# Row scatters without their pacing waits, and expert biases loaded as rows and turned on TensorE, in an attention and mixture-of-experts layer

## What is computed

```python
x = layernorm(x + attention(x))          # 8 heads of 64, causal, gated per head
x = layernorm(x + ffn(x))
# ffn: 16 experts with hidden width 256, two chosen for each token, and a shared network of width 512
logits = x @ Wg;  gates = softmax over the two largest logits
y = sum over chosen e: gates[e] * ((silu(x @ W1[e] + b1[e]) * (x @ W11[e] + b11[e])) @ W2[e] + b2[e])
z = silu(x @ Ws1 + bs1) * (x @ Ws11 + bs11) @ Ws2 + bs2
ffn = y + z
```

## Time and profile before

| | |
|---|---|
| time, median of 3 runs | 671.99 us (671.56 to 672.36) |
| time of the profiled execution | 674.43 us |
| its span, first to last instruction | 672.7 us |
| PE busy | 626.1 us (93%) |
| DVE, ACT, POOL busy | 456.1, 387.4, 176.8 us |
| shared network, first product to last | about 491 to 559 us of the span |
| experts | about 559 to 645 us |

### The profile page before, as it was taken

One profiled execution on the slowest core, in us unless ns is written; L12 is line 12 of the kernel. 1 busy time (PEld: TensorE's weight loads), 2 busy tenths in 40 slices (PEclk: granted clock), 3 DMA queues, 4 the chain that ended last, 5 costly groups with the idle time before them and its releaser, 6 DMA issues.

```text
span 672.7 us, 14853 instructions
## 1 busy us (share of the span) xinstructions
PE 626.1 (93%) x5286; PEld 506.0 (75%) x5286; DVE 456.1 (68%) x1493; ACT 387.4 (58%) x821; POOL 176.8 (26%) x302
## 2 busy tenths in 40 slices
PE   7899999999999999999999999999996979888865
PEld 5688888778888877888887788888754548778752
DVE  5977767677776767777676787767684355556524
ACT  6766556676655667665566766556551114656643
POOL 5211101231110122111012211101336633666640
PEclk9999999999999999999999999999997979999997
DMA  7499961179970119993011200000293112222224
GB/s 156 109 168 158 167 96 33 34 145 167 174 116 2 32 33 66 4 5 2 1 34 32 64 1 2 2 1 1 75 313 49 43 33 71 72 71 73 63 66 153
DMA packets 112920, 48.55 MB, mean 72 GB/s; under 512 B 53712, under 2 KB 106192, under 8 KB 112848
## 3 DMA queue, kind: packets, MB, share of 16 engines
q1 hardware_dynamic: 109456, 42.20, 43.0%
q0 software_dynamic: 2560, 5.28, 2.3%
q10 hardware_dynamic: 832, 0.14, 0.1%
HBM read 14.78 MB, written 24.43 MB: 58 GB/s over the span
## 4 chain that ended last, share of the span: by engine, by line
PE 81%; DVE 8%; ACT 4%; issue 2%; another core or an unknown queue 2%; DMA 1%; DVEq 0%; ACTq 0%; POOLq 0%; POOL 0%; SPq 0%
PE ps_o L1304 19%; PE ps_t L1166 18%; PE ps_s L1270 10%; PE ps_s L1272 9%; PE ps_s L1438 6%; PE ps_o L1426 3%; PE ps_s L1348 2%; PE ps_o L1166 2%; PE ps_o L1316 2%; PE ps_s L1177 2%; PE ps_s L1174 2%; PE ps_t L1362 2%; DVE q_hl L821 1%; PE ps_s L1456 1%
## 5 line engine op out<-in xcount | busy, mean ns | idle before, releaser
L1166 PE MATMUL ps_t<-ident,probs 128*128 128x128 f32 x1104 | 172.8, 273 | 4.8 <-ACT probsT L690 2.0
L1166 PEld LDWEIGHTS ps_t<-ident,probs 128*128 128x128 f32 x1104 | 135.8, 140 | 43.8 <-issue 8.3
L679 ACT ACTIVATE probs<-probs,nmax 128x128 f32<-128x128 f32 (+15 forms) x128 | 153.4, 1199 | 22.9 <-DVE nmax L977 15.9
L986 DVE COPY probsT<-ps_t 128x512 f32<-128x512 f32 (+3 forms) x160 | 91.2, 570 | 100.5 <-PE ps_t L1166 99.2
L690 ACT ACTIVATE probsT<-ps_t 128x512 f32<-128x512 f32 (+3 forms) x160 | 89.3, 558 | 95.3 <-PE ps_t L1166 94.1
L1270 PE MATMUL ps_s<-k_h,q_hl 128*128 128x512 f32 (+3 forms) x320 | 141.0, 444 | 0.4 <-DVE q_hl L821 0.4
L1304 PE MATMUL ps_o<-probsT,v_sb 128*64 128x128 f32 x2176 | 140.0, 277 | 0.1
L549 POOL TENSOR_TENSOR rden<-rsum,minus_one 128x2 f32<-128x2 f32 x64 | 44.3, 693 | 348.8 <-ACT probs L679 337.6
L972 DVE TENSOR_SCALAR_CACHE_REDUCE probs<-ps_s 128x512 f32<-128x512 f32 x192 | 127.7, 686 | 0.3 <-issue 0.3
L1304 PEld LDWEIGHTS ps_o<-probsT,v_sb 128*64 128x64 f32 x2176 | 116.8, 137 | 14.5 <-issue 12.5
L1272 PE MATMUL ps_s<-k_l,q_hl 128*128 128x512 f32 (+3 forms) x320 | 116.9, 366 | 0.0
(11 more groups left out here) (172 smaller groups left out, 735.5 us busy)
## 6 DMA issues: line engine op xcount, KB each, us to landing
x_sorted<-zeros SPq DMA_DIRECT2D x68, 258.0 KB, 9.0
k_h<-k_h SPq DMA_DIRECT2D x32, 128.0 KB, 2.3
k_l<-k_l SPq DMA_DIRECT2D x32, 128.0 KB, 2.3
w_all<-in_L_ffn_W SPq DMA_DIRECT2D x2, 2048.0 KB
xg<-x_sorted SPq DMA_DIRECT2D x48, 65.0 KB
act_s<-y_rows SPq DMA_DIRECT2D x3, 512.0 KB, 5.4
x_acc<-in_L_attn_tokens SPq DMA_DIRECT2D x4, 256.0 KB, 4.4
y_rows<-y_sb,row_all POOLq DMA_INDIRECT x48
```

What stands on the lines that cost most here:

```text
L679: nc.scalar.activation(probs[s % 2][h][:, 0:w], probs[s % 2][h][:, 0:w], ACT.Exp, bias=nmax[:, row], scale=-1.0, accum_out=rsum[:, row]).t ...
L986: nc.vector.tensor_copy(probsT[s % 2][h][:, c * BT:c * BT + w // P, :].rearrange("p n i -> p (n i)"), ps_t[1][:, 0:w]).then_inc(moved1, 1)
L1166: return nc.tensor.transpose(dst, src, ident[:, :])
```

## The change

It does two things. GpSimd's waits for `act_done` ahead of the scatters go, with their table; the waits for the set's rows, gates and places stay. And the experts' biases come as two transfers of rows (16 experts on 16 partitions, 256 numbers each, `b_rows`) near the start of SyncE's queue. TensorE turns them in 4 small transposes after product 2, and VectorE copies the 64 columns from PSUM into `w_all` at its own place after product 2. The 32 transfers of single numbers and VectorE's wait for them go.

```diff
-    SCATTERED_AT = (1, 2, 3, 4, 5, 6, 6, 7, 8, 9, 9, 10, 11, 12, 13, 14)
+        b_rows = sb("b_rows", [E, 2, H], f32)
...
+            for a, b in enumerate((b1, b11)):
+                sp.dma_start(b_rows[:, a, :], b).then_inc(bias_in, 16)
             sp.wait_ge(b2_set, 2)
...
-            with nc.allow_non_contiguous_dma("a column of biases of each block of hidden values, 16 KB"):
-                for a, b in enumerate((b1, b11)):
-                    for e in range(E):
-                        sp.dma_start(w_all[:, e, UP + a * HB:UP + (a + 1) * HB],
-                                     b[e].rearrange("(m p) -> p m", p=P)).then_inc(bcol_in, 16)
...
-                for j, t in enumerate(tiles):
-
-                    pool.wait_ge(act_done, SCATTERED_AT[i * HALF + j])
+                for t in tiles:
                     for k in range(TOPK):
                         nc.gpsimd.indirect_dma_start(
...
+            def expert_biases():
+
+                dve.wait_ge(bias_psum, 1)
+                nc.vector.tensor_copy(w_all[:, :, UP:UP + 2 * HB], ps_t[0][:, 0:2 * HB * E].rearrange("p (c e) -> p e c", e=E))
...
                 elif n == 2:
+                    expert_biases()
                     norm("norm", n3)
...
-            dve.wait_ge(bcol_in, 16 * 2 * E)
...
+            def turn_biases():
+                pe.wait_ge(bias_in, 32)
+                pe.wait_ge(moved0, ONE + PAIRS * (GROUPS // 2))
+                for a in range(2):
+                    for m in range(HB):
+                        at = (a * HB + m) * E
+                        mm = nc.tensor.transpose(ps_t[0][:, at:at + E], b_rows[:, a, m * P:(m + 1) * P], ident[0:E, 0:E])
+                mm.then_inc(bias_psum, 1)
...
             for n in range(2, NC * SB):
                 shared_up(n)
+                if n == 2:
+                    turn_biases()
```

More of the change, by code:

```diff
@@ L325, in attention_moe_layer @@
         dve_step, act_step = sem("dve_step"), sem("act_step")
-        bcol_in = sem("bcol_in")
+        bias_in, bias_psum = sem("bias_in"), sem("bias_psum")
         ms_ready, std_ready, rms_ready, xn_ready, xnT_ready, tT_ready = (sem(n) for n in (
```

## The result

The changed kernel takes **676.07 us** (674.1 to 677.84, 6 runs) where the kernel before took 671.77 us (670.75 to 673.06, 6 runs) beside it: ratio 1.0057, interval 1.0039 to 1.0076. It is 4.3 us slower by the medians. The forecast had it 10.7 us slower. The profiled execution, one of the six, took 675.38 us, with a span of 673.6 us and TensorE 93% busy, as before.

The account below looks back on a forecast made before the run. Bound: TensorE's chain, idling while unbroken GpSimd scatters hold words between engines. Terms: 10.6 (later experts) + 0 (bias transfers) + 0.1 (new instructions) = 10.7 us slower, 682.7 us; range 679 to 687, down to 664 for 8 in 10.

Parts of the forecast that it names:

- The reading of the trace: Between 498 and 559 us, some 7 to 8 us of unbroken scatters hold words between other engines until the string ends.
- the rival that the recording makes them: Holds come from writing the profile, so timed runs stay near 672 us; one of two no-effect ways, together 0.13.
- The step that failed: First string without waits ends at 519.2, ScalarE gets product 6 at about 520.9 instead of 512.73: 8.2 us later.
- My written test: ScalarE taking product 6 before 515 with scatters still running, or a `shared_down(0)` before 525, would prove the reading wrong.
- The second string: 16 scatters from 529.2 to 549.1, words through at about 550.8, first turn of the experts 10.6 us later at 569.2.
- The bias transfers: 32 SyncE issues and 8192 packets of 4 bytes gone from about 498 to 520: gain 0, bounds 0 and 7.5 us.
- The new instructions: Four transposes, 0.5 us while TensorE waits anyway, and VectorE's copy, 0.25 us: 0.1 us taken on the path.
- The sum against the profiled execution: 10.7 us added to the profiled 674.43 gives 685.1; the median of runs lies 2.4 lower, so 682.7 us.
- a leaking hold: Words get through now and then inside a long string: 1.5 to 8 us slower, middle 676.5; chance 0.14.
- Hold of its own length: Holds end after some 4 to 6 us regardless of scatters: 672 within 1.3; one of two no-effect ways, together 0.13.
- the sign of the forecast: Whole kernel slower by more than 0.2% (1.3 us): chance 0.64, against 0.09 for the same and 0.27 for faster.

Follow-up runs that it names:

- r_before: The kernel before, unchanged, run again on an occasion without holds: 642.08 us, ratio 1.0001.
- e2_waits_only: The kernel before with only GpSimd's pacing waits removed, biases still as 32 transfers of single numbers: 676.77 us, ratio 1.0082.
- s_short_rows: The changed kernel with scatters bringing 64 bytes of each row instead of 520, experts working on empty rows: 677.02 us, ratio 1.0074.
- e7: The changed kernel with a 0.33 us GpSimd fill behind each scatter of set 1 only: 662.80 us, ratio 0.9890.
- e5: The changed kernel with a fill of 8 columns behind every scatter, scatters 1.36 us apart: 676.60 us, ratio 1.0105.
- e6: The changed kernel with a 0.33 us GpSimd fill behind each scatter of set 0 only: 664.72 us, ratio 0.9912.

## Why the prediction was right in its sign and wrong in its size

**The reading of the trace** stood in part. The holds come with GpSimd's scatters, and taking the pacing waits away costs: 5.4 us alone. But they are not only late words between engines, since TensorE also paused between rows of one `shared_down` and VectorE on its own last step. And the rival that the recording makes them is weaker than it was, not out. The forecast set timed against profiled executions, but the profiled 675.38 us is one of the six timed ones, and each timed execution on record has a span and a granted clock of its own, so none is known to have run unrecorded. What speaks against the rival is that the same program, recorded in the same way, shows no hold in r_before (641.69 us profiled). That the recording takes part beside the scatters was not tested.

**The step that failed** is the one that the forecast took for its largest term: the first string "now goes on past its 10th scatter ... so the string ends at 519.2 and the words go through 1.1 to 2.05 us later, at about 520.9 ... a shift of 8.2 us". The rule behind it, that words go through only after a string has ended, was read from three strings whose ends and the holds' ends lay together. In e2_waits_only, the same program but for the waits, the word comes at 512.74 with scatters running to 519.4. With that the rest of the term was too large too: `slots_ready` moved by 1.2 us (3.8 in e2_waits_only, 524.30 for 520.55), not by 8.2, and the second string began 6 us earlier than forecast. My written test, ScalarE taking product 6 before 515 with scatters running, was met and named the reading wrong. There the product was taken 0.55 us after it was made.

**The second string** went as forecast but for its place: 16 scatters, a hold over its later part, and words at 2.9 us after its end (1.7 taken, 1.1 to 2.05 the bounds). The same 2.9 us came in e2 (545.17, 548.10) and s_short_rows (542.83, 545.81). The forecast let TensorE stand from 544.2 to 552.3, 8.1 us; it stood 8.51, where it had been 4.41. That the two agree so well is luck: the forecast had product 13 behind the hold, and TensorE made it before (its rows from 534.37 to 538.3 are products 12 and 13), while the word came 1.2 us later behind the string than was taken. This is the part of the mechanism that makes the changed kernel slower, and e7, which spaces only this string, removes it, on an occasion with holds.

**The bias transfers** were taken at 0, with bounds of 0 and 7.5 us. Measured: 1.1 to 1.3 us, at the edge of what can be told. Their packets do take part in the first hold (product 6 at 512.7 in two traces with them, 509.3 to 510.7 in four without), which the forecast held against the third string, where there were none. Both are so: scatters hold alone, and the packets add 2 to 3.4 us there. The gain is small because TensorE's pauses in the first string mostly change places (3.50 + 1.11 + 1.87 = 6.5 us for 5.73).

**The new instructions**: the four transposes took 0.41 us and the copy 0.21 us, where 0.5 and 0.25 were taken.

**The sum against the profiled execution** hid an uncertainty. From the first turn of `xg` to the end the kernel before took 114.05 us in its profile and the changed one 111.6 (673.6 - 561.99). My reading is that the same delays reach into the experts and vary there; the six spans of the changed kernel go from 672.4 to 676.1 us. So a difference of 3.3 us at the first turn is 0.9 in the spans and 4.3 in the medians. The forecast took this stage as fixed.

**The rival** of a leaking hold, 1.5 to 8 us slower with 676.5 as its middle, is the one that came: 676.07. It had 0.14. What spoke for it, a word that got through after 1 us at 507.8, was in the rows; I weighed the three ends that agreed more heavily. That its middle was hit within half a microsecond is luck: it was the middle of a wide range, without a working behind it. "Hold of its own length" of 4 to 6 us is out for the second string, where a product was held 9.7 us, and no single length fits all traces (15.7 us in e5; at most 10.85 in the kernel before, from ScalarE's start at 531.45 to the next at 542.30).

**No rival said that the size depends on the occasion**, and that is the largest miss. Where no word is held, the change costs 0.1% (643.01 for 642.22 us, interval 1.0003 to 1.0021), and taking only the waits away costs nothing that can be told (0.9999). There ScalarE takes product 6 at 508.8, within 0.1 us of its making; in the other traces a product was taken up to 17.0 us late. So the sign of the forecast was right for an occasion with holds, and nothing in the prediction said that it needed one.

## What stays open

I did not find which part of the chip is held, nor what differs between the occasions. The chip number in the record was 0, 6 and 9 with holds and 9 and 3 without, so a chip is not of one kind. Whether something else was running beside this core can't be seen in a one-core trace. Whether the recording of the profile takes part is open too. Each kernel left one trace on an occasion, so how the holds fall from execution to execution is not known. Whether writing descriptors or their packets do it was not separated, and why 1.36 us apart was worse than 1.265 was not tried again. A string's age alone doesn't decide either: in e6 a product went through 10.3 us into an unbroken string, in the kernel before one made 9.7 us into it was held.

## What to carry to other kernels

A wait that costs its own engine 16.7 us can be worth 5 us to the kernel, or nothing, by the occasion, if that engine issues indirect transfers back to back: before taking such pacing away, look for words that arrive late while GpSimd scatters, and space the scatters instead of pacing them by other engines' progress. Spacing one of the two strings made this kernel 1.1% faster on an occasion with holds (662.8 us) and 1.1% slower on one without (649.1): no version here beats the kernel before on both, so such a gain must be measured on more than one occasion. Forecasting which instruction a hold will fall on went wrong twice here, in the first string and in e6. And an event that ends together with another three times is still only seen together: the cheapest experiment, the one edit alone, told it.

## What the runs showed of the hardware that I had not expected

- The same program took 642.2 us or 670 to 672 us on different occasions, without any difference up to its first indirect scatter at 499 us; 14.7 us of it lie before the first sorted tile and 18 behind it.
- On the second kind of occasion, 32 scatters at 1.36 us from one to the next held ScalarE's word for 15.7 us; at 1.57 us none was held, in four kernels.
- In such holds an engine also pauses where its program has no wait: TensorE 0.97 us between the two passes of one matmul (e6), 1.87 us inside a `shared_down` (the changed kernel).
- Scatters with an eighth of the bytes held the others as long (ScalarE's start 2.98 us after the string's end, 2.9 with full rows).
- With the 8192 packets of 4 bytes product 6 came 2 to 3.4 us later beside scatters at 1.265 us, and no later beside scatters at 1.57 us.
